# A selective-scan kernel in which softplus is summed in two halves and the product with C is taken per unit

## The reference, cut to what matters

```python
def step(h, inp):
    u_l, d_l, B_l, C_l = inp
    dA = jnp.exp(d_l[..., None] * A)
    h = h * dA + (d_l * u_l)[..., None] * B_l[:, :, None, :]
    y = jnp.einsum('bkdn,bkn->bkd', h, C_l)
    return (h, y)
...
dts = jnp.einsum('bkrl,kdr->bkdl', dts, dt_w)
delta = jax.nn.softplus(dts + dt_b[None, :, :, None])
A = -jnp.exp(A_logs).reshape(K, DN, N)
ys = _selective_scan(xs, delta, A, Bs, Cs, Ds.reshape(K, DN))
y = (y0 + y1 + y2 + y3).transpose(0, 2, 1)
y = _ln(y, outnorm_g, outnorm_b).reshape(Bc, Hc, Wc, DN)
y = y * jax.nn.silu(z)
return y @ out_proj_w
```

## Time and profile before

| | |
|---|---|
| runs | 31033.51, 31037.8, 31046.34 us |
| profiled execution: its span, the one time that it has | 31035.4 us |
| PE busy | 28615.5 us (92%) |
| DVE busy | 27602.9 us (89%) |
| POOL busy | 25853.7 us (83%; in layer 1 over 90%) |
| ACT busy | 24152.4 us (78%) |
| mean granted clock of TensorE | 0.991 |
| HBM | 89 GB/s over the span |

### The profile page before, as it was taken

One profiled execution on the slowest core, in us unless ns is written; L12 is line 12 of the kernel. 1 busy time (PEld: TensorE's weight loads), 2 busy tenths in 40 slices (PEclk: granted clock), 3 DMA queues, 4 the chain that ended last, 5 costly groups with the idle time before them and its releaser, 6 DMA issues.

```text
span 31035.4 us, 986155 instructions
## 1 busy us (share of the span) xinstructions
PE 28615.5 (92%) x399070; PEld 10807.2 (35%) x399070; DVE 27602.9 (89%) x18447; ACT 24152.4 (78%) x37826; POOL 25853.7 (83%) x13288
## 2 busy tenths in 40 slices
PE   8999799999999999999999999999999999999998
PEld 2333233333333333333333333333333333333333
DVE  7888799999999999999999999999999999999998
ACT  4555688888888888888888888888888888888887
POOL 0000599999999999999999999999999999999999
PEclk9999999999999999999999999999999999999999
DMA  3333344444444444444444444444444444444444
GB/s 82 88 84 82 79 103 99 102 98 102 99 101 100 100 100 100 101 100 102 99 102 100 101 99 101 99 103 98 103 98 102 100 102 99 102 98 102 98 102 90
DMA packets 3821867, 3043.32 MB, mean 98 GB/s; under 512 B 2184848, under 2 KB 2987792, under 8 KB 3796944
## 3 DMA queue, kind: packets, MB, share of 16 engines
q1 hardware_dynamic: 3809888, 2910.77, 44.4%
q0 software_dynamic: 8560, 77.41, 0.7%
HBM read 2325.71 MB, written 449.58 MB: 89 GB/s over the span
## 4 chain that ended last, share of the span: by engine, by line
PE 28%; POOL 20%; issue 18%; ACT 13%; DVE 8%; DMA 1%; POOLq 0%; SPq 0%; ACTq 0%; DVEq 0%
POOL state L942 17%; PE dbu L1032 9%; PE pp L1126 7%; DVE state L1477 5%; ACT state L1256 5%; PE yb L1051 4%; DVE dg L1467 2%; PE pp L1100 2%; POOL dd L949 2%; PE pp L1089 1%; PE pp L1120 1%; ACT sp_w L1333 1%; POOL dd L962 1%; ACT sp_v L1334 1%; PE b_t L1068 1%
## 5 line engine op out<-in xcount | busy, mean ns | idle before, releaser
L942 POOL TENSOR_TENSOR state<-state,cc 128x1024 f32<-128x1024 f32 x9408 | 22044.2, 2375 | 1411.5 <-DVE state L1477 1381.9
L1477 DVE TENSOR_TENSOR_SCAN state<-state,dbu 128x1024 f32<-128x1024 f32 x9408 | 21000.9, 2269 | 2295.8 <-PE dbu L1032 2292.6
L1256 ACT ACTIVATE state<-dl,a_neg 128x512 f32<-128x512 f32 x18816 | 12250.6, 711 | 21.2 <-DMA dl<-dlx 1.4
L1032 PE MATMUL dbu<-dg,du_t 64*32 64x256 f32 x301056 | 10198.2, 383 | 968.5 <-DVE state L1477 895.6
L1032 PEld LDWEIGHTS dbu<-dg,du_t 64*32 64x32 f32 x301056 | 5100.0, 106 | 7276.9 <-issue 6198.1
L1051 PE MATMUL yb<-state,mask 128*32 128x512 f32 x37632 | 5078.5, 612 | 2.2 <-POOL state L942 2.2
L1467 DVE TENSOR_TENSOR dg<-b_t,mask_q 128x1024 f32<-128x1024 f32 x3136 | 3757.7, 1198 | 41.4 <-PE b_t L1068 41.4
L229 POOL DMA_DIRECT2D act_d<-acted x32 | 16.3, 509 | 3218.2 <-DVE mixed L489 2909.2
L1126 PE MATMUL pp<-sp_a,minus 128*128 128x512 f32 x2352 | 1321.4, 644 | 587.4 <-ACT ye L1284 252.1
L1339 ACT ACTIVATE sp_y<-pp 128x512 f32<-128x512 f32 x1176 | 704.2, 599 | 1440.4 <-PE pp L1126 1417.1
L437 DVE SCALAR_TENSOR_TENSOR acc<-image,cw_v,acc 96x432 f32<-96x432 f32 (+2 forms) x2912 | 1687.6, 647 | 0.0
(11 more groups left out here) (174 smaller groups left out, 26584.2 us busy)
## 6 DMA issues: line engine op xcount, KB each, us to landing
dl<-dlx SPq DMA_DIRECT2D x4704, 256.0 KB, 4.7
cc<-cd SPq DMA_DIRECT2D x3136, 256.0 KB, 6.2
dlx<-dd SPq DMA_DIRECT2D x1176, 256.0 KB, 2.0
shifted<-in_x SPq DMA_DIRECT2D x384, 392.0 KB, 12.5
xs<-ye SPq DMA_DIRECT2D x1176, 112.0 KB, 2.8
xs<-ye SPq DMA_DIRECT2D x588, 128.0 KB, 2.6
image<-in_x SPq DMA_DIRECT2D x32, 1176.0 KB, 24.5
act_d<-acted POOLq DMA_DIRECT2D x32, 1176.0 KB, 9.1
```

The source lines that it names most:

```text
L942: nc.gpsimd.tensor_tensor(its, its, cc[:, h, s, :], ALU.mult).then_inc(hc_done, 1)
L1032: last = nc.tensor.matmul(dst[:, :, TQ * e:TQ * e + TQ], du_t[its, j, col:col + JC], dg[its, h, 2 * k + s, MG * TQ * g:MG * TQ * g + MG * ...
L1256: nc.scalar.activation(state[:, slot, :, m * WPX:m * WPX + WPX].rearrange("p (q k) t -> p q k t", k=2), by_place(dl[:, J // 2, 2 * h + J % ...
L1477: nc.vector.tensor_tensor_scan(its, its, dbu[p % 2][:], 0.0, ALU.mult, ALU.add).then_inc(scan_done, 1)
```

## The change

1. `exponent` and `small_part` are cut into two halves of 256 columns (L_SUMS = 3 and 5), with two uses of the bank (`m..` and `n..`); PP has 39 uses.
2. PP and the tables of steps are new. LAG is 6, L_U is 4.
3. `times_c` takes a whole unit (2048 columns) after the scan of its second step.
4. `reset` is gone. The first place of each window in `dlx` is written once, at the start, and SP writes only the other 63 places.
5. The last exponential of a chain goes into `sp_w` and `sp_r` has two buffers. `softplus` waits for nothing on POOL any more; `logarithms` does.
6. Products over 64 rows of contraction (`skip_l`, `xp_l`, `mean_y`, `out_l`) now go over 128 rows, the added ones with zero weights.
7. SP's order: `both_halves(b, 1, 2)` and `c_out(b, 1)` come earlier. ACT has two more waits (`xd_out`, `gate_in`).

```diff
-ROOT_RESET = 2.0 ** 45
+RESET = 2.0 ** 90
...
-PP = [("d01", 0), ("cen", 1), ("m02", 0), ("var", 1), ("s10", 0), ("d02", 0), ("m10", 0), ("xin0", 1),
...
-      ("yout", -1), ("s01", 1), ("d00", 1), ("z0", 1), ("m01", 1), ("xd1", 1), ("z1", 1), ("yf0", 0), ("s02", 1)]
+PP = [("d01", 0), ("m02", 0), ("cen", 1), ("n02", 0), ("var", 1), ("s10", 0), ("xin0", 1), ("d02", 0),
...
+      ("d00", 1), ("z0", 1), ("m01", 1), ("z1", 1), ("n01", 1), ("s02", 1), ("yf0", 0)]
...
-    {46: (0, 0), 18: (-1, 1)}, 25, 27, 28, 30, 32, [33, 34], 35, 38, 40)
-S_XIN, S_CONV, S_SILU, S_XD, S_Z = [11, 16], [21, 24], 27, [32, 44], [42, 45]
+    {19: (-1, 1), 47: (0, 0)}, 26, 28, 28, 30, 32, [32, 32], 35, 39, 41)
+S_XIN, S_CONV, S_SILU, S_XD, S_Z = [7, 13], [22, 25], 26, [32, 34], [43, 44]
...
-CHAINS = [(5, 1, 0), (12, 1, 1), (19, 1, 2), (33, 0, 0), (40, 0, 1), (47, 0, 2)]
-DUT = {13: (0, 1, 0), 20: (0, 1, 1), 27: (0, 1, 2), 41: (1, 0, 0), 0: (0, 0, 1), 7: (0, 0, 2)}
-L_LOG, L_SUM, L_U = 1, 3, 5
+CHAINS = [(6, 1, 0), (12, 1, 1), (18, 1, 2), (33, 0, 0), (40, 0, 1), (46, 0, 2)]
+DUT = {0: (0, 0, 1), 8: (0, 0, 2), 14: (0, 1, 0), 20: (0, 1, 1), 28: (0, 1, 2), 42: (1, 0, 0)}
+L_LOG, L_SUMS, L_U = 1, (3, 5), 4
+SUM_COLS = TOK // 2
...
-AHEAD, LAG = 4, 5
+AHEAD, LAG = 4, 6
...
-        skip_l = sb("skip_l", [JB, NJ, JB])
+        skip_l = sb("skip_l", [128, NJ, JB])
...
-        sp_r = sb("sp_r", [128, TOK])
+        sp_r = sb("sp_r", [128, 2, TOK])
...
+                            sp.dma_start(dlx[f, j].rearrange("p (w t) -> p w t", t=WPX)[:, :, 0:1],
+                                         resets[:].unsqueeze(2)).then_inc(resets_in, 16)
...
-                    sp.wait_ge(reset_done, c + 1)
-                    sp.dma_start(dlx[f, j], dd[:, 0, :]).then_inc(dl_out, 16)
+                    sp.wait_ge(dl_done, c + 1)
+                    sp.dma_start(inner(dlx[f, j]), inner(dd[:, 0, :])).then_inc(dl_out, 16)
+                    if later(T * 2 + f):
+                        sp.wait_ge(da_done, (T * 2 + f) * (UPP * MG) + (4 * j + 4 - UPP) * MG)
...
+                    if s == 0:
+                        return
...
-                    its = state[:, slot, WPS * s:WPS * s + WPS, :].rearrange("p w x -> p (w x)")
-                    nc.gpsimd.tensor_tensor(its, its, cc[:, h, s, :], ALU.mult).then_inc(hc_done, 1)
+                    its = state[:, slot, :, :].rearrange("p w x -> p (w x)")
+                    nc.gpsimd.tensor_tensor(its, its, cc[:, h, :, :].rearrange("p s x -> p (s x)"),
+                                            ALU.mult).then_inc(hc_done, 1)
...
-                def reset(T, f, j):
...
-                    nc.gpsimd.tensor_tensor(dd[:, 0, 0::WPX], resets[:], resets[:], ALU.mult).then_inc(reset_done, 1)
...
-                    last = nc.tensor.matmul(pp[:], xp_l[0:JB, f, 1, :], u[0:JB, 2, :], start=False, stop=True)
+                    last = nc.tensor.matmul(pp[:], xp_l[:, f, 1, :], u[:, 2, :], start=False, stop=True)
...
-                        last = nc.tensor.matmul(pp[:], minus[:, i, :], part[:], start=i == 0, stop=i == 2)
+                        last = nc.tensor.matmul(pp[:, cols], minus[:, i, :], part[:, cols], start=i == 0, stop=i == 2)
...
-                    nc.scalar.activation(sp_y[:], pp[:], ACT.Exp).then_inc(pp_read, 1)
+                    nc.scalar.activation(sp_w[:, cols], pp[:, cols], ACT.Exp).then_inc(pp_read, 1)
```

More of the change, by code:

```diff
@@ L646, in layer1 @@
             sem(n + "_1") for n in "act_in ln_done rs_done shifts u_done z_done".split()]
-        (sp_exp, sp_act, dl_done, hd_done, reset_done) = [
-            sem(n + "_1") for n in "sp_exp sp_act dl_done hd_done reset_done".split()]
+        (sp_exp, sp_act, dl_done, hd_done, resets_in) = [
+            sem(n + "_1") for n in "sp_exp sp_act dl_done hd_done resets_in".split()]
         dl_out = sem("dl_out")
@@ L777, in _ @@
                 assert len(loads) == N_WLOADS
+                sp.wait_ge(consts, N_CONSTS)
+                with nc.allow_non_contiguous_dma(reason="the first step of each window, once"):
+                    for f in range(2):
+                        for j in range(NJ):
+                            sp.dma_start(dlx[f, j].rearrange("p (w t) -> p w t", t=WPX)[:, :, 0:1],
+                                         resets[:].unsqueeze(2)).then_inc(resets_in, 16)
+                sp.wait_ge(resets_in, 2 * NJ * 16)
                 def load_act(T):
@@ L986, in body @@
                             times_u(T, f, j)
-                            reset(T, f, j)
                         if p == S_GATED and has(b - 1):
@@ L1057, in sum_states @@
                                                     skip_l[:, J // 2, JC * (J % 2):JC * (J % 2) + JC],
-                                                    u[0:JB, J // 2, its], start=False, stop=False)
+                                                    u[:, J // 2, its], start=False, stop=False)
                     last.then_inc(ysum_done, 1)
@@ L1146, in y_mean @@
                     free_bank(b, "ymean")
-                    for part, (rows, _) in enumerate(PARTS):
-                        last = nc.tensor.matmul(pp[:], mean_y[0:rows, :], yf[0:rows, part, :], start=part == 0, stop=part == 1)
+                    for part in range(2):
+                        last = nc.tensor.matmul(pp[:], mean_y[:, part, :], yf[:, part, :], start=part == 0, stop=part == 1)
                     last.then_inc(pp_ready, 1)
@@ L1153, in y_var @@
                     pe.wait_ge(ysq_done, b)
-                    for part, (rows, _) in enumerate(PARTS):
-                        last = nc.tensor.matmul(pp[:], mean_y[0:rows, :], ye1[0:rows, 2 + part, :], start=part == 0,
+                    for part in range(2):
+                        last = nc.tensor.matmul(pp[:], mean_y[:, part, :], ye1[:, 2 + part, :], start=part == 0,
                                                 stop=part == 1)
@@ L1161, in y_out @@
                     pe.wait_ge(g_done, b)
-                    for part, (rows, _) in enumerate(PARTS):
-                        last = nc.tensor.matmul(pp[0:C, :], out_l[0:rows, part, :], yf[0:rows, part, :], start=part == 0,
+                    for part in range(2):
+                        last = nc.tensor.matmul(pp[0:C, :], out_l[:, part, :], yf[:, part, :], start=part == 0,
                                                 stop=part == 1)
@@ L1193, in front @@
                         steps_of(b, f, j)
-                    for T, f, j in chains_at(b, p, L_SUM):
-                        exponent(b, T, f, j)
+                    for half in range(2):
+                        for T, f, j in chains_at(b, p, L_SUMS[half]):
+                            exponent(b, T, f, j, half)
                     if p in DUT:
@@ L1314, in gate_in @@
                     act.wait_ge(pp_ready, uses_before(b, f"z{part}") + 1)
+                    if has(b):
+                        act.wait_ge(z_done, b + 1)
                     nc.scalar.activation(zi[0:rows, part, :], pp[0:rows, :], ACT.Identity,
@@ L1322, in softplus @@
                     act.wait_ge(pp_ready, use + 1)
-                    if later(c):
-                        act.wait_ge(dl_done, c)
                     nc.scalar.activation(sp_a[:], pp[:], ACT.Abs)
-                    nc.scalar.activation(sp_r[:], pp[:], ACT.Relu).then_inc(pp_read, 1)
+                    nc.scalar.activation(sp_r[:, (f + j) % 2, :], pp[:], ACT.Relu).then_inc(pp_read, 1)
                     act.wait_ge(pp_read, use + 1)
@@ L1409, in body @@
                             softplus(b, f, j)
-                        for T, f, j in chains_at(b, p, L_SUM):
-                            small_part(b, T, f, j)
+                        for half in range(2):
+                            for T, f, j in chains_at(b, p, L_SUMS[half]):
+                                small_part(b, T, f, j, half)
                         if p in DUT:
@@ L1425, in body @@
                                 y_squares(b)
-                            if p in S_AFFINE:
-                                y_affine(b, S_AFFINE.index(p))
+                            for part in range(2):
+                                if p == S_AFFINE[part]:
+                                    y_affine(b, part)
                         if p == S_SILU:
```

68 lines of the change are left out of this document (37 added, 31 removed), and 5 rows, old and new, of the table PP.

## The result

The changed kernel takes 30534.04 us (median; 30517.93 to 30536.2), the ratio to the kernel before is 0.9836 [0.982, 0.9851]: 504 us or 1.6% faster, 2.6 us per tile. The forecast was 602 us.

What follows compares the result with a forecast made beforehand. POOL was taken to bound over half of a tile, PE's long steps the rest. Terms -3.25 - 1.35 + 0.15 + 0 + 1.3 = -3.15 us per tile, -617 us, +15 once: 30,436 us; range 29,950 to 31,080, own range 30,100 to 30,850.

Steps and rivals of the forecast that it cites:

- the share of 0.61: Part of a tile in which POOL leads, 86 of 140 us; POOL's savings were counted at this share.
- the rival in which POOL leads everywhere: All 5.3 us saved on POOL count: -5.2 us per tile, 30,030 us; chance 0.20.
- The wait of softplus: ACT's Abs no longer waits for POOL's step size: -1.35 us per tile, next to none expected at the first logarithm.
- Halves: PE's sums cut in two: 0.19 us more six times, +1.15 on PE; gain from shorter steps 0, bounds 0 to -3.1.
- 128 rows: PE's product pairs without change of form, five times: -0.75 us per tile on PE, which leads in 0.39 of it.
- The new order: New order of PE's bank uses: new waits of PE, together +1.3 us per tile.
- the output projection: PE's next bank use waits for DVE's scan and read, up to 1.8 us: +1.0 per tile, bounds 0 and 1.8.
- The half sum behind the gate: Gate's product and a half sum share step 43, losing 1.02 us of cover on PE: +0.3, bounds 0 and 1.0.
- the longer write: SP's write of 252 bytes at a time adds up to 4.3 us before ACT's step 44; costed at nothing.
- -3.25 for POOL: Product with C per unit (-3.3) and no reset (-2.0), 5.3 us per tile from POOL, counted at 0.61.
- That PE is the bound: Rival: POOL's gain becomes waiting for scans, PE's 130 us stay: +0.1 per tile, 31,070 us; chance 0.11.
- The new wait on POOL: Rival: POOL's step size waits 2.2 us for the second half sum; 31,325 us in three chains, 32,600 in six; chance 0.15.

Runs made afterwards that it cites:

- the fourth of those runs: Changed kernel with product per step, old buffers and the reset on POOL put back, leaving new order, halves and 128 rows: 31550.56 us, 1.0162.

## Why the prediction came out right, and where it was wrong

**What bounded the kernel.** The step that failed is the share of 0.61: "POOL leads in 86 of 140 us", read from where the chain of waits runs. Removing POOL's work gave +86 and -2 us, not the 3.25 us per tile (637 us) that were put down for it. The chain ran through POOL because Abs waited for it once per tile; with that wait gone it runs there 2% of the time. The share was also one tile's, with the pieces that the chain calls "issue" counted to POOL: the page gave POOL 20% of the whole run's chain, and "issue" 18%. The 7 us per tile for which POOL waited for scans had been read, and were used only against the rival in which POOL leads everywhere. They spoke against the forecast as well. The durations were right: 4565 ns for 4561, and POOL's busy time, in the stretch of the earlier trace rows:

```profile
20000.00:21400.00 1400.00, 1309.66 (x20176) 572.16 (x20174) 1298.36 (x712) 1170.70 (x1904) 1285.89 (x375) 1.00 0.52 103
```

A tile is 137.75 us, so the 1400 us hold 10.16 and POOL is busy 126.5 us in one. The 137.75 us lie inside the 135 to 139 outside of which the prediction was to count as wrong.

**The wait of softplus.** -1.35 put down, 0.77 measured alone and 0.9 in the changed kernel. Sign and mechanism right, the size too large: the wait was counted in full, where PE felt 0.77 us of it.

**Halves.** Put down as 0, with bounds 0 to -3.1; measured 1.96 us per tile, 383 us, the largest of the parts that were undone one at a time. The reason given for 0, that a saved wait of DVE is worth nothing if PE is late at the next step, did not hold: between the long steps PE was early and waited for DVE. The sign that was named, DVE's wait below 9 us, did not quite come: it fell to 9.1 us, from 12.0 with whole sums. The price was put at +0.19 per sum from 1.48 us each; start to start it is 1.49 (20034.62 - 20033.13), so two halves take 2.98 us where a whole sum takes 2.77 in the kernel with whole sums, 0.21 more, or 1.3 us per tile for the 1.15 put down:

```profile
20033.13 0.70 PE L1138 MATMUL pp<-sp_a,minus 128*128 128x256 f32 x2
20033.67 0.59 PE L1138 MATMUL pp<-sp_w,minus 128*128 128x256 f32 x2
20034.10 0.59 PE L1138 MATMUL pp<-sp_v,minus 128*128 128x256 f32 x2
20034.62 1.98 PE L1043 MATMUL dbu<-dg,du_t 64*32 64x256 f32 x64
```

The 0.9 us per tile that the overhead in the Trainium skill (TensorEngine Tiling, Instruction Overhead) would have added are not seen here: the middle product of 256 columns takes 0.43 us from its start to the next (20034.10 - 20033.67), half of the 0.86 us of the one of 512, so nothing is left that comes once per product. (With that overhead the prediction's sum gives 30,612 us, not 30,620.) That PE's busy time is only 74 us higher with halves than with whole sums says less, since the granted clocks differ, 0.993 and 0.989.

**128 rows.** -0.75 on PE, counted at 0.39, so -0.3; measured 1.86 us of PE's work and 1.2 us of time. By the groups above a pair of `mean_y` saves 0.26 us and the two of `xp_l` together 0.21 (178.0 / 79 - 163.4 / 80), where 0.15 each was put down; `out_l` saves 0.24, and `skip_l`, which the sum left out, 0.14; what of the 1.86 us the groups do not show is not assigned to a line. PE's work counted at 0.65, not at 0.39.

**The new order.** +1.0 for the output projection was wrong in its mechanism: PE starts the chain's first product without a wait, since DVE is early and reads at once:

```profile
20119.54 0.75 DVE L1518 SCALAR_TENSOR_TENSOR xa<-pp,alp,xa 96x512 f32<-96x512 f32 x1 [0.44 <-PE pp L1175]
```

PE's next inputs, 20119.33 to 20120.36, cover that read. The half sum behind the gate waits 0.85 us (68.3 / 80) in place of 0.7, so +0.15 and not +0.3. In their place came two waits that had not been named: `xa`, 1.05, and the `xp_l` product behind Relu, 1.25. The first sits in SP's queue, which the prediction followed for `dlx` alone; the longer write had been put down at nothing. The write of `dlx`, 3.2 us where it was 2.0, stands ahead of that load:

```profile
20002.58 0.54 SPq L838 DMA_DIRECT2D dlx<-dd  x1
20005.78 1.74 SPq L843 DMA_DIRECT2D dl<-dlx  x4
20007.80 0.34 SPq L790 DMA_DIRECT2D xa<-act_d  x1
```

The second goes when `S_AFFINE` is moved.

**The sum.** Removed one at a time from the changed kernel, the product is worth 170 us, the buffers 177, the halves 383, the rows 238: 968 us, against a gain of 504. The rest, -464 us or 2.4 us per tile, would be the price of the new order with what remains, if parts added up; they do not, as the fourth of those runs shows. The forecast's -3.25 for POOL and its 0 for the halves were wrong in opposite directions by amounts of the same order, and so the sum came out within 100 us of the measured gain. That is luck. The range has no better ground: added up, the bounds of the terms reach from some 29,160 to some 31,190 us, and the prediction's 30,100 to 30,850 us does not come out of them.

**The rivals.** That PE is the bound had the right reading of POOL (its gain turns into waits for scans) and the wrong time, 31,070 us, since it gave the halves nothing. The new wait on POOL came, 4.71 us at one place and 8.9 per tile, between the 6.6 of three chains and the 13.2 of six at 2.2 each. In order of time:

```profile
20001.29 1.27 POOL L969 TENSOR_TENSOR dd<-sp_r,sp_w 128x512 f32<-128x512 f32 x1 [4.71 <-ACT sp_w L1357]
```

No slower kernel came of it, for the reason given against it: a POOL that waits is not the bound. Slower came where POOL was not relieved, with order, halves and rows alone, and there through Abs, `cc` and `xa`.

**Still open.** Why the kernel with order, halves and rows alone loses 1016 us, where product and buffers put back singly cost 170 and 177. The three waits that it shows have SP's queue and POOL's step size in common, but the reset on POOL in the new order was not tried alone, and neither was the pair of product and buffers. How much of it is the lower granted clock (0.986) and how much the waits was not taken apart. The new order was not separated from LAG and L_U.

## What to carry to other kernels

An engine that stands on the chain of waits, or is the busiest, is not the bound while it waits several us per tile for another: take its work away by itself before it is given a share of the gain. Where engines within a few per cent of each other hand over through two buffers, the longest single step costs more than its share of the work, so cutting it up can pay even when it adds work. When the step of one engine moves, follow every transfer that stands behind its semaphore in the queue that issues it.

## What was unexpected of the hardware

- Writing 63 of 64 columns, in pieces of 252 bytes, takes 3.2 to 3.4 us to land where whole rows take 2.0; 6.3 had been estimated from the transfers of 112 KB. The number of bytes is the same but for 1.6%. In the old order it cost no time (no reset alone: 1.0 [0.999, 1.001]); in the changed kernel it stands ahead of the load of `xa`, for which PE waits.
- The transfers of 112 KB, which nothing in the change touches but the step of their issue, went from 2.8 us to 6.1 (4.2 with whole sums). The writes in short pieces are not the reason: with whole rows in the new order it is 6.1 as well, and without the reset in the old order 2.9. What sets their time was not tried. In the page of the changed kernel:

```profile
dlx<-dd SPq DMA_DIRECT2D x1176, 252.0 KB, 3.2
...
xs<-ye SPq DMA_DIRECT2D x1176, 112.0 KB, 6.1
```

- On POOL, 512, 1024 and 2048 columns take 1281, 2375 and 4565 ns: 1094 and 1095 ns for each further 512, a straight line, with 187 ns (1281 - 1094) that come once per instruction. As the products follow each other, some 50 of these 187 ns were hidden before, and no more: that a unit would save 0.14 us had been read from the spacing, and POOL's busy time fell by 683 us where the product alone was changed, 3.5 us per tile for 3.3 put down.
